# Second attention: two key tiles of exponentials summed by accumulating transfers instead of Pool, one part fewer for PE

## The reference

```python
qk = jnp.einsum('bhqd,bhkd->bhqk', q, k)
emb_matrix = sinusoidal_embeddings(length, d_head)
indices = jnp.arange(length)[:, None] - jnp.arange(length) + length - 1
embeddings = emb_matrix[indices]
qe = jnp.einsum('bhqd,qkd->bhqk', q, embeddings)
weights = jax.nn.softmax((qk + qe) / jnp.sqrt(jnp.float32(d_head)), axis=-1)
output = jnp.einsum('bhqk,bhkd->bhqd', weights, v)
```

## Time and profile before

| | |
|---|---|
| time, median of 3 runs | 2847.14 us (2841.78 to 2848.37) |
| profiled execution | 2855.66 us, its span 2853.8 us |
| PE busy over the span | 2481.0 us (87%) |
| DVE, POOL, ACT busy | 1991.5, 1967.8, 1402.8 us |
| second attention, first to last score product (L1118) | 1508.4 to 2454.6 us |

### The profile page before, as it was taken

The page is one execution under the profiler, slowest core; times in us unless marked ns, Lnnn a source line. Parts: engine busy times, 40 slices in busy tenths (PEclk is TensorE's granted clock), DMA queues, the critical chain, the costliest instruction groups (busy, mean ns, idle before and its releaser), DMA issues. The chain is left out here.

```text
span 2853.8 us, 47289 instructions
## 1 busy us (share of the span) xinstructions
PE 2481.0 (87%) x18516; PEld 817.5 (29%) x18516; DVE 1991.5 (70%) x3075; ACT 1402.8 (49%) x2548; POOL 1967.8 (69%) x763
## 2 busy tenths in 40 slices
PE   7899999999999999968988999999999999651255
PEld 2564222222222222235552222222222222240144
DVE  4475787787787787647886777877778777277134
ACT  3345555555555555523335565665656656440012
POOL 3114788888888888844446888888888888630763
PEclk9999999999999999989999999999999999775568
DMA  4994222322222322039764321223212230350337
GB/s 80 238 237 137 49 50 49 76 67 49 53 49 55 80 57 53 9 134 308 231 216 116 74 64 49 64 71 90 64 49 64 71 75 16 102 180 9 96 121 248
DMA packets 236267, 278.16 MB, mean 97 GB/s; under 512 B 65392, under 2 KB 171376, under 8 KB 232842
## 3 DMA queue, kind: packets, MB, share of 16 engines
q1 hardware_dynamic: 225548, 249.89, 32.3%
q0 software_dynamic: 6144, 16.85, 1.9%
q10 hardware_dynamic: 4352, 8.39, 0.8%
HBM read 165.17 MB, written 110.67 MB: 97 GB/s over the span
## 5 line engine op out<-in xcount | busy, mean ns | idle before, releaser
L854 POOL TENSOR_TENSOR room_af<-room_af 128x2048 f32<-128x2048 f32 x160 | 725.6, 4535 | 163.6 <-ACT room_af L826 149.8
L1229 POOL TENSOR_TENSOR bias<-bias 128x2048 f32<-128x2048 f32 x160 | 724.3, 4527 | 153.3 <-ACT bias L1199 134.1
L826 ACT ACTIVATE room_af<-PS 128x512 f32<-128x512 f32 x1024 | 555.9, 594 | 396.3 <-PE PS L748 396.3
L1199 ACT ACTIVATE bias<-PS 128x512 f32<-128x512 f32 x1024 | 555.9, 594 | 376.2 <-PE PS L1123 373.8
L635 DVE CUSTOM_DVE_ANT_0 PS<-PS,bias 128x1024 f32<-128x1024 f32 x512 | 620.1, 1241 | 160.6 <-PE PS L623 142.6
L1004 DVE TENSOR_REDUCE row_min_kf<-PS 128x1 f32<-128x1024 f32 x512 | 601.9, 1220 | 107.2 <-PE PS L996 98.6
L1118 PE MATMUL PS<-stacks_kf 128*128 128x512 f16 x1024 | 339.2, 387 | 15.3 <-PEq L90 8.5
L741 PE MATMUL PS<-QS_af,KS_af 128*128 128x512 f16 x1024 | 334.5, 387 | 14.3 <-PEq L90 4.5
L774 PE MATMUL PS<-room_af,V_af 128*32 128x512 f32 x2048 | 272.7, 605 | 1.2 <-ACT room_af L826 1.2
L1143 PE MATMUL PS<-bias,V_kf 128*32 128x512 f32 x2048 | 272.8, 605 | 0.2 <-ACT bias L1199 0.2
L748 PE MATMUL PS<-turned_bias,eyes 64*32 64x512 f16 x4096 | 210.6, 388 | 0.0
(11 more groups left out here) (184 smaller groups left out, 3070.4 us busy)
## 6 DMA issues: line engine op xcount, KB each, us to landing
query_key_halves<-bias SPq DMA_DIRECT2D x32, 768.0 KB, 4.0
query_key_halves<-room_af SPq DMA_DIRECT2D x32, 512.0 KB
stacks_kf<-query_key_halves SPq DMA_DIRECT2D x64, 256.0 KB, 7.2
KS_af<-query_key_halves SPq DMA_DIRECT2D x48, 256.0 KB, 4.8
QS_af<-query_key_halves SPq DMA_DIRECT2D x48, 256.0 KB, 7.0
lows_kf<-query_key_halves SPq DMA_DIRECT2D x96, 128.0 KB
token_rows<-rows_t SPq DMA_DIRECT2D x16, 514.0 KB, 4.2
FT_t<-token_rows SPq DMA_DIRECT2D x16, 514.0 KB
```

Source lines behind the costliest of these rows:

```text
L826: nc.scalar.activation(prob[:, n % PR, head, :], score_ps[s % 3], ACT.Exp).then_inc(exps, 1)
L854: nc.gpsimd.tensor_tensor(acc[:, u % 2], so_far, prob[:, n % PR], ALU.add).then_inc(acc_ok, 1)
L1199: nc.scalar.activation(prob[:, n % PR, j, :], score_ps[s % 3], ACT.Exp, scale=-1.0 / (W1S * W1S)).then_inc(exps, 1)
L1229: nc.gpsimd.tensor_tensor(acc[:, u % 2], so_far, prob[:, n % PR], ALU.add).then_inc(acc_ok, 1)
```

## The change

The ring has 5 tiles and no longer holds tile 0, whose exponentials ACT writes straight into a new buffer `sums` (2 places of one tile). Tiles 1 and 2 are added into `sums` by transfers that POOL issues with an accumulating addition; the second is issued only when the first has landed. POOL adds tiles 3 to 6 in three additions into `acc` (one place now) and then `acc` into `sums`, a fourth addition, at step 0 of the next unit. PE sums two parts, tile 7 and `sums`, in step 3 of the next unit instead of step 1. The reciprocals move to steps 4 to 7, and `finish` of a unit to step 0 of the second unit after it. ACT waits for the transfers where it reuses the places of tiles 1 and 2.

```diff
-                PR = 4
-                o1, o2 = HG * CH * PR, HG * CH * (PR + 2)
-                prob = zf[:, 0:o1].rearrange("p (r j n) -> p r j n", r=PR, j=HG)
-                acc = zf[:, o1:o2].rearrange("p (r j n) -> p r j n", r=2, j=HG)
+                PR = 5
+                o1, o2 = HG * CH * PR, HG * CH * (PR + 1)
+                ring = zf[:, 0:o1].rearrange("p (r j n) -> p r j n", r=PR, j=HG)
+                acc = zf[:, o1:o2].rearrange("p (j n) -> p j n", j=HG)
+                sums = tile("sums", [P, 2, HG, CH], F32)
...
-                ADDS = KTU - 3
+                MOVED = 2
+                LASTS = 1
+                ADDS = KTU - 1 - MOVED - LASTS
+                STEPS = KTU - 1
+
+                def prob(n):
+                    u, kt = divmod(n, KTU)
+                    return sums[:, u % 2] if kt == 0 else ring[:, (u * STEPS + kt - 1) % PR]
...
-                DEN, REC, TAKE, FIN = 1, 2, 1, 5
+                DEN, REC, TAKE, FIN = 3, 4, 1, 0
...
-                                parts = [prob[:, (KTU * u + kt) % PR] for kt in range(ADDS + 1, KTU)] + [acc[:, u % 2]]
+                                parts = [prob(KTU * u + kt) for kt in range(KTU - LASTS, KTU)] + [sums[:, u % 2]]
...
+                                u, kt = divmod(n, KTU)
+                                if kt == 0 and j == 0 and u >= 2:
+                                    act.wait_ge(max_full, job_at[(u - 2, "den")] + 1)
+                                if kt >= 1 and j == 0 and u * STEPS + kt - 1 >= PR:
+                                    u, kt = divmod(u * STEPS + kt - 1 - PR, STEPS)
+                                    act.wait_ge(weighed, KTU * u + kt + 2)
+                                    if kt < MOVED:
+                                        act.wait_ge(moved, 16 * (MOVED * u + kt + 1))
+                                    elif kt + 1 < KTU - LASTS:
+                                        act.wait_ge(acc_ok, ADDS * u + max(kt - MOVED, 1))
                                     else:
                                         act.wait_ge(max_full, job_at[(u, "den")] + 1)
...
+                            def move_tile(n):
+                                u, kt = divmod(n, KTU)
+                                pool.wait_ge(exps, HG * (n + 1))
+                                if kt == 1:
+                                    pool.wait_ge(weighed, KTU * u + 1)
+                                if MOVED * u + kt >= 2:
+                                    pool.wait_ge(moved, 16 * (MOVED * u + kt - 1))
+                                nc.gpsimd.dma_start(sums[:, u % 2].rearrange("p j n -> p (j n)"), prob(n).rearrange("p j n -> p (j n)"),
+                                                    accum_op=ALU.add).then_inc(moved, 16)
...
+                            def add_sums(u):
+                                pool.wait_ge(moved, 16 * MOVED * (u + 1))
+                                pool.wait_ge(acc_ok, ADDS * (u + 1) - 1)
+                                nc.gpsimd.tensor_tensor(sums[:, u % 2], sums[:, u % 2], acc, ALU.add).then_inc(acc_ok, 1)
+
+                            LATE_ADD, SUMMED, BACK = KTU - LASTS - 1, 0, 2
+                            for n in range(NU * KTU + 2):
+                                u, kt = divmod(n, KTU)
+                                if n < NU * KTU and 1 <= kt <= MOVED:
+                                    move_tile(n)
+                                if n < NU * KTU and MOVED + 2 <= kt <= LATE_ADD:
+                                    add_tile(n)
+                                if kt == SUMMED and u >= 1:
+                                    add_sums(u - 1)
+                                if u < NU and kt == FIN and u >= BACK:
+                                    finish(u - BACK)
+                            for u in range(NU - BACK, NU):
+                                finish(u)
```

More of the change, by code:

```diff
@@ L934, in attention_keys_first @@
                 LOADS = 16 * 14
-                ADDS = KTU - 3
+                MOVED = 2
[5 more added lines that the diff above has]
+                    return sums[:, u % 2] if kt == 0 else ring[:, (u * STEPS + kt - 1) % PR]
                 sems = [ssem(n) for n in ("stk0", "stk1", "v_in0", "v_in1", "x_in0", "x_in1", "out_st0", "out_st1", "m_in0",
                                           "m_in1", "emb_in", "high_in", "fill", "max_full", "max_read", "full", "exps", "weighed",
-                                          "acc_ok", "recd", "taken", "scaled", "fin")]
+                                          "acc_ok", "moved", "recd", "taken", "scaled", "fin")]
                 (stk0, stk1, v_in0, v_in1, x_in0, x_in1, out_st0, out_st1, m_in0, m_in1, emb_in, high_in, fill, max_full, max_read,
-                 full, exps, weighed, acc_ok, recd, taken, scaled, fin) = sems
+                 full, exps, weighed, acc_ok, moved, recd, taken, scaled, fin) = sems
                 stk, v_in, x_in, out_st, m_in = (stk0, stk1), (v_in0, v_in1), (x_in0, x_in1), (out_st0, out_st1), (m_in0, m_in1)
@@ L1144, in weigh @@
                                                             V[:, bb % 2, kt, (g * HG + j) * D:(g * HG + j + 1) * D],
-                                                            prob[:, n % PR, j, :], start=(kt == 0), stop=(kt == KTU - 1),
+                                                            prob(n)[:, j, :], start=(kt == 0), stop=(kt == KTU - 1),
                                                             skip_group_check=True)
@@ L1198, in _ @@
                                 act.wait_ge(full, s + 1)
-                                nc.scalar.activation(prob[:, n % PR, j, :], score_ps[s % 3], ACT.Exp,
+                                nc.scalar.activation(prob(n)[:, j, :], score_ps[s % 3], ACT.Exp,
                                                      scale=-1.0 / (W1S * W1S)).then_inc(exps, 1)
@@ L1218, in add_tile @@
                             def add_tile(n):
                                 u, kt = divmod(n, KTU)
-                                if kt == 0 or kt > ADDS:
-                                    return
                                 pool.wait_ge(exps, HG * (n + 1))
[L1224 to L1235, removed]
+                                first = kt == MOVED + 2
@@ new lines, in add_tile @@
+                                done = ADDS * u + kt - MOVED - 2
+                                if done >= 1:
+                                    pool.wait_ge(acc_ok, done)
+                                nc.gpsimd.tensor_tensor(acc, prob(n - 1) if first else acc, prob(n), ALU.add).then_inc(acc_ok, 1)
+                            def add_sums(u):
+                                pool.wait_ge(moved, 16 * MOVED * (u + 1))
+                                pool.wait_ge(acc_ok, ADDS * (u + 1) - 1)
+                                nc.gpsimd.tensor_tensor(sums[:, u % 2], sums[:, u % 2], acc, ALU.add).then_inc(acc_ok, 1)
@@ L1250, in _ @@
                             for n in range(NU * KTU + REC + PIECES):
-                                u, piece = n // KTU - 1, n % KTU - REC
+                                u = n // KTU - 1
                                 if u >= 0 and n % KTU == DEN:
                                     take_sums(job_at[(u, "den")], u)
+                                u, piece = divmod(n - REC, KTU)
+                                u -= 1
                                 if n < NU * KTU:
```

## The result

The changed kernel takes 2880.66 us (median of 4 runs, 2879.7 to 2886.18), the kernel before 2846.84 us in the same comparison. The ratio is 1.0126, with a 95% interval of 1.0108 to 1.0144: slower by 33.8 us, where 37 were forecast. The profiled execution took 2886.18 us.

What follows compares the result with a forecast made beforehand. PE bounds the kernel before; after the change POOL's line with one exposed landing would, at 30.7 us per unit. 32 us for 32 units plus 4.5 of tail make 37, on the median 2847: 2884 us, range 2822 to 2965.

Steps and rivals of the forecast that it cites:

- The period: POOL's time per unit in the second attention: 30.7 us, 1.0 over the 29.7 before, 32 us for 32 units.
- 24.1: POOL's work per unit in us: additions 18.7, finish with gaps 2.8, two transfer issues 2.6.
- W: Wait on POOL from the end of the first transfer's issue to its landing, taken as 5.9 us.
- loads: SP's loads in every second unit delay the first transfer; 0 to 1.5 us per unit over all, 0.7 taken.
- The landing: First accumulating transfer of a unit: lands 7.2 us from its issue, the middle of 6.2 and 8.2.
- the second 2.2: Extra us in an accumulating 1 MB transfer for reading the place it adds to, on top of 2.2 of moving.
- 6.8 and 4.4 us: Estimates of the transfer's landing from a fit of 2 us and 436 GB/s, with two reads and with one.
- PE's gain: One part less in PE's sums: 0.9 us per unit, 29 us over 32 units if PE keeps the pace.
- PE stays the bound: Rival: transfer lands within 6.0 us of issue, undisturbed by loads; unit 28.8, -24 us, 2823 us; chance 0.24.
- The tail: Stage's end after the last exponential: 11.6 us instead of 7.7; 4 us later, 5 if POOL is late, 4.5 taken.
- The clock: PE's granted clock might fall in its waits, but stood at 1.00 with PE busy 6.66 of 10 us.
- The waits: POOL never waits for ACT before tile 4; PE's gaps go back through ACT to the second landing, or to POOL.

Runs made afterwards that it cites:

- experiment 2: The changed kernel with a sixth place in the ring, so tile 7 no longer waits for the second landing; 2872.3 us, ratio 1.0089 to the kernel before.
- experiment 3: The changed kernel with only tile 1 added by transfer, POOL making five additions and PE still summing two parts; 2836.28 us, ratio 0.9964 to the kernel before.
- Experiment 4: The changed kernel with both transfers as plain copies without addition, so tiles 0 and 1 are missing from the sum; 2837.0 us, ratio 0.9968 to the kernel before.
- Experiment 9: experiment 5 with the row maxima and their small transfers one step earlier; 2850.57 us, ratio 1.0014 to the kernel before.
- Experiment 6: The kernel before with PE's sums in step 2 instead of 1, a ring of five and reciprocals one step later; 2857.48 us, ratio 1.0029.
- experiment 5: The changed kernel with a ring of six and the second transfer issued behind POOL's addition of tile 4; 2905.04 us, ratio 1.0204 to the kernel before.
- experiment 8: experiment 5 with POOL adding tile 7 too, PE summing one part, and add_sums behind the next unit's first issue; 2856.3 us, ratio 1.0033 to the kernel before.
- experiment 12: experiment 10 with SP's result store and residual load issued one unit later; 2826.56 us, ratio 0.9936 to the kernel before.
- experiment 10: experiment 8 with the row maxima and their small transfers one step earlier; 2859.78 us, ratio 1.0048 to the kernel before.
- experiment 1: The changed kernel with finish between the two transfer issues instead of ahead of the first; 2866.04 us, ratio 1.0078 to the kernel before.

## Why the prediction was right, and where its sizes were off

The mechanism is the one forecast: POOL's work in a line with one exposed landing becomes the period of the stage. Experiments 2, 3 and 4 show it from three sides. Removing ACT's stall leaves the round (30.3), while removing the second transfer, and with it the exposed landing, or taking the addition out of the transfers gives PE the pace back (29.15 and no loss). Experiments 3 and 4 also lessen the traffic. Experiment 9 doesn't: it keeps both transfers and all additions, fills the wait with the addition of tile 4, and most of its units last 29.15 too. Point by point:

**The period.** 24.1 + W + loads made 30.7, and 30.70 was measured. That they agree so closely is luck, for two terms are off by 0.7 us each, against each other. POOL's own work without the first issue was put at 22.8 and is 22.1. The issue takes 0.86 us in place of 1.3, and the next addition starts 0.58 after the issue's start (1993.52, 1994.10), inside it. From the first issue to the second were forecast 1.3 + 5.9 + 0.7 = 7.9, and measured are 8.6: 7.47 undisturbed in place of 7.2, and 1.1 of late landings in place of 0.7. Of the 1.1 only 0.9 are the loads that the prediction named.

**The landing.** 7.2 us from the issue were taken, as the middle between 6.2 and 8.2; the median is 7.0. No row of before told the middle from the ends, and each of these us is worth 32 in the sum, so this too had luck in it. The packets of one transfer are under way for some 5 us, as windows of 1 us show:

```profile
1987.00:1988.00 1.00, 1.00 (x13) 0.12 (x3) 0.02 (x1) 0.26 (x1) 0.00 (x0) 1.00 0.65 131
1988.00:1989.00 1.00, 1.00 (x8) 0.21 (x6) 0.67 (x1) 0.19 (x1) 0.00 (x0) 1.00 1.31 262
...
1992.00:1993.00 1.00, 1.00 (x8) 0.25 (x10) 1.00 (x2) 0.54 (x2) 0.00 (x0) 1.00 0.06 8
```

Experiment 4's plain copy lands after 4.6, so the addition costs 2.4, against the second 2.2 of the prediction. The prediction put it down to a second read. The packets' 5.2 us against 2.7 fit that, but no run separates the read from the addition itself, and the trace counts the same bytes for both. The Trainium skill, "Collectives: The Full Stack", section "The bandwidth ceiling: the fold count and why AG ≠ RS ≠ AR", says that the two reads, and not the addition, halve the rate. The trace agrees as far as the rate goes, 5.2 to 2.7 us. The estimates from the Trainium skill, "DMA: Bandwidth & Descriptors", section "Anatomy of one DMA — SWDGE (gpsimd) path", 6.8 and 4.4 us, agree as well, with 7.0 and 4.6.

**PE's gain.** 0.9 us was too much: it is 0.56. The difference of steps for the parts themselves came out (the step from 2013.33 to 2018.33 takes 5.00 us in place of 5.86), but the move of the sums from step 1 to step 3, a part that the prediction neither priced nor named among what it costed at nothing, uncovers ACT's output copy. The step ahead of it, between value products, then takes 3.71 us in place of 3.33:

```profile
2006.29 1.06 PE L1153 MATMUL PS<-bias,V_kf 128*32 128x512 f32 x8
2010.00 1.07 PE L1153 MATMUL PS<-sums_kf,V_kf 128*32 128x512 f32 x8 [0.30 <-issue]
2013.33 1.07 PE L1153 MATMUL PS<-bias,V_kf 128*32 128x512 f32 x8
2018.33 1.06 PE L1153 MATMUL PS<-bias,V_kf 128*32 128x512 f32 x8
```

Experiment 6 shows the same cost alone. It didn't touch the forecast, since POOL was the bound, but it touches the rival "PE stays the bound". That one would have ended near 2837 us, as experiments 3 and 4 did, and not at 2823.

**The tail.** Forecast 4.5 us, measured 5.5. From the last exponentials' end to that of the sums it is 2505.61 - 2492.39 = 13.2 us, where it was 7.7:

```profile
2491.31 1.08 ACT L1213 ACTIVATE bias<-PS 128x512 f32<-128x512 f32 x2 [0.31 <-PE PS L1133]
...
2502.41 1.93 PE L1165 MATMUL PS<-bias,den_w_kf 128*32 128x512 f32 x8 [7.69 <-POOL sums_kf L1256]
2504.09 1.52 PE L1165 MATMUL PS<-sums_kf,den_w_kf 128*32 128x512 f32 x8
```

The two parts, at a granted clock of 0.50, take 3.2 us (2.9 forecast); the rest is POOL's lateness.

**The sum in the stage.** From the first score product to the end of its exponentials the first unit takes 33.8 us, where it took 28.0. Its first transfer runs beside the loads of the stage's begin, and its D is 15.45 us. No term of the prediction stands for these 5.8 us. The other 31 units take 27.1 us more than before, counted by their exponentials, and the tail 5.5: 38.4 in all, where the prediction had 32 and 4.5. The medians differ by 33.8. The two profiled executions lie 5.5 and 8.8 us over their medians, which is as much as such a difference leaves uncertain.

**The clock.** The prediction argued that it would not fall in waits of 2 to 4 us. It did (0.75 and 0.82 in two windows of 4 us above, 0.50 within them). The row that it leaned on, 6.66 of 10 us busy at 1.00, was no guide. The lower clock cost little, because POOL had the pace: experiment 2, without ACT's stalls, is still slower than before by 0.9%.

**The waits.** Nearly as forecast ("never"), POOL waits for ACT ahead of its additions only twice, 3.0 us in all, and PE's gaps go back through ACT to the second landing (59.2 us of ACT's waits in 23 times). The row maxima, the late transfer of experiments 5 and 8, play no part in the changed kernel itself: no wait for them stands among its waits.

## What to carry to other kernels

An addition moved from an engine to an accumulating transfer lost time here as long as the issuing engine stood still for its landing; ask for each such wait what independent work can stand in it (experiment 12 fills 13.9 us that way), and price the landing with the addition (7.0 us here, where the plain copy took 4.6). When the pace of a stage sits within 1 us of a second engine's, price every move, also those that "don't change the work": an instruction that is taken away may have been the cover of another one (ACT's copy, 0.32 us per unit). Load on the transfer engines is not free either: look at which small transfers (the maxima) and which bulk loads (the keys) come beside the new ones, since they were what ate the gain in experiments 5, 8 and 10: the maxima in the first two, the keys in the last.

## What the hardware showed beyond expectation

- Transfers of 1 KB that bring the row maxima, for which PE never waits in the kernel before, held PE up 52.8 us in 29 units of experiment 5 when they ran beside a 1 MB accumulating transfer, and not at all in experiment 9, where they are asked for a step earlier.
- The distance D from the issue of a transfer to the next, which waits for its landing, goes from 7.45 to 11.5 us in one kernel, the first unit left out, and to 14.1 in experiment 1, where the transfer starts 2.6 us earlier.
- An accumulating transfer of 1 MB with neither a load nor a store nor a packet of the instruction queues beside it landed after 6.91 to 7.22 us in every run. With such packets and no load it took up to 9.3. The two go together in time; no run tests whether one causes the other.
- PE's granted clock was 0.50 right after a wait of 2.47 us in an otherwise full stage.
